# A two-layer graph network on one NeuronCore: the edge phase in four steps per group, written as functions, with the phases that follow it reordered

## The reference, cut to what matters

```python
def L0(V, E, edge_index):            # 8 heads of 16
    Q, K, Vv = V[src] @ Wq + bq, V[dst] @ Wk + bk, V[dst] @ Wv + bv
    scores = einsum(Q, K) / 4 + (E @ Wb + bb)
    alpha = exp(scores - segment_max(scores, dst)[dst]) / segment_sum(...)[dst]
    return segment_sum(alpha * Vv, dst) @ Wo + bo
def L1(x, W, a, edge_index):
    h = x @ W
    e = leaky_relu((h @ a1)[src] + (h @ a2)[dst], 0.2)
    return segment_sum(softmax(e)[:, None] * h[src], dst)   # one softmax over all edges
x = layernorm(x + L0(x, edge_attr, edge_index))
x = layernorm(x + L1(x, W, a, edge_index))
```

## Time and profile before

| | |
|---|---|
| median of 3 executions | 1305.71 us (1303.69 to 1308.90) |
| profiled execution | 1310.51 us, its span 1308.8 us |
| granted clock of PE | 0.737 |
| busy: PE, DVE, ACT, POOL | 733.0, 776.4, 703.8, 787.1 us |
| moved by DMA | 196.96 MB, 150 GB/s on the mean |
| edge phase, second phase, third phase | to 675, to 981, to 1309 us |

### The profile page before, as it was taken

The page is one execution under the profiler, slowest core; times in us unless marked ns, Lnnn a source line. Parts: engine busy times, 40 slices in busy tenths (PEclk is TensorE's granted clock), DMA queues, the critical chain, the costliest instruction groups (busy, mean ns, idle before and its releaser), DMA issues.

```text
span 1308.8 us, 16204 instructions
## 1 busy us (share of the span) xinstructions
PE 733.0 (56%) x3263; PEld 501.9 (38%) x3263; DVE 776.4 (59%) x4008; ACT 703.8 (54%) x2047; POOL 787.1 (60%) x803
## 2 busy tenths in 40 slices
PE   2167767766766676677524555455456453453540
PEld 1045555545544454555524445455452111111110
DVE  2367667776766776678734555555527565464651
ACT  0257767767777687688512333333355454354542
POOL 7677666666766676660036665566643666556665
PEclk9577787778778877877756776777767666666775
DMA  5246556565465655656143767767643222222210
GB/s 138 67 124 209 179 182 198 168 226 176 155 215 181 195 172 179 206 164 234 65 147 119 215 214 213 213 210 221 209 138 121 63 79 71 69 66 71 76 47 26
DMA packets 81840, 196.96 MB, mean 150 GB/s; under 512 B 19746, under 2 KB 21815, under 8 KB 81732
## 3 DMA queue, kind: packets, MB, share of 16 engines
q1 hardware_dynamic: 56558, 148.29, 35.2%
q0 software_dynamic: 25184, 47.65, 12.4%
HBM read 122.71 MB, written 77.22 MB: 153 GB/s over the span
## 4 chain that ended last, share of the span: by engine, by line
ACT 36%; another core or an unknown queue 28%; issue 17%; DVE 12%; PE 6%; POOL 1%; ACTq 0%; POOLq 0%; DVEq 0%
ACT h_res L642 9%; ACT node_out L642 8%; ACT yb L642 7%; DVE node_out L1152 3%; PE psum L599 3%; DVE part L1158 2%; DVE nst L1164 2%; ACT h_res L693 2%; ACT xsT L764 2%; ACT h_res L664 2%; ACT h_res L745 1%; PE psum L606 1%; ACT h_res L651 1%; ACT xsT L740 1%
## 5 line engine op out<-in xcount | busy, mean ns | idle before, releaser
L442 POOL DMA_INDIRECT out_dram<-yb,at_last x196 | 195.0, 995 | 134.6 <-ACT yb L642 75.3
L438 POOL DMA_INDIRECT xs<-in_x,src_tab x196 | 187.1, 955 | 126.1 <-remote 76.0
L438 POOL DMA_INDIRECT xs<-x_all,row_tab x196 | 187.4, 956 | 111.4 <-remote 56.4
L438 POOL DMA_INDIRECT h_res<-in_x,dst_tab x196 | 212.4, 1084 | 59.7 <-issue 59.7
L532 PE MATMUL psum<-xsT,h_res 128*128 128x512 f32 x98 | 93.2, 1051 | 155.0 <-ACT h_res L693 155.0
L627 PE MATMUL psum<-node_out,ident_inv 128*128 128x512 f32 x98 | 80.8, 919 | 149.1 <-DVE node_out L1152 105.3
L642 ACT ACTIVATE h_res<-node_in,shift,rstd 128x128 f32<-128x128 f32 (+1 forms) x392 | 155.8, 486 | 6.3 <-DVE shift L907 3.6
L599 PE MATMUL psum<-w,xsT 128*128 128x129 f32 x392 | 85.5, 386 | 110.3 <-ACT xsT L740 109.7
L740 ACT ACTIVATE xsT<-psum 128x512 f32<-128x512 f32 x49 | 29.3, 597 | 206.6 <-remote 125.5
L599 PEld LDWEIGHTS psum<-w,xsT 128*128 128x128 f32 x392 | 75.8, 287 | 118.5 <-ACT xsT L740 116.7
L642 ACT ACTIVATE yb<-psum,shift,rstd 128x128 f32<-128x128 f32 x196 | 73.8, 457 | 67.4 <-remote 33.5
(11 more groups left out here) (253 smaller groups left out, 1988.5 us busy)
## 6 DMA issues: line engine op xcount, KB each, us to landing
x1d_in<-x_all SPq DMA_DIRECT2D x98, 256.0 KB
node_in<-in_x SPq DMA_DIRECT2D x48, 512.0 KB
x_all<-h_res SPq DMA_DIRECT2D x48, 512.0 KB
out_dram<-node_out SPq DMA_DIRECT2D x48, 512.0 KB
x_all<-yb SPq DMA_DIRECT2D x49, 256.0 KB
src_b<-src_t SPq DMA_DIRECT2D x49, 256.0 KB
node_in<-x_all SPq DMA_DIRECT2D x24, 512.0 KB
h_res<-in_edge_attr SPq DMA_DIRECT2D x7, 784.0 KB
```

The lines of the kernel that those rows point to most:

```text
L438: return pool.indirect_dma_start(out=to, out_offset=None, in_=table, in_offset=bass.IndirectOffsetOnAxis(ap=idx, axis=0))
L442: return pool.indirect_dma_start(out=table, out_offset=bass.IndirectOffsetOnAxis(ap=idx, axis=0), in_=rows, in_offset=None, bounds_check=l ...
```

## The change

The loop over steps with its offsets is taken apart into functions, one for each piece of work, and every engine's order is written anew. A group takes four steps: in step s its transposes, q, k, queries, products, values and scores; in s+1 maxima, exponentials, sums, shares and weighted transposes; in s+2 outputs, addition and bn_stats; in s+3 bn_aggr, logarithm, shift and scaling. The number of bn_aggr stays: 4 rows and 8 of a node chunk, twelve in a step. Node chunks run 3 steps ahead of the groups (`FIRST` = -3), the bias for them lies in PSUM, chunk 0 is moved by two transfers (96 and 10 partitions). The transposes signal `xs_T` and `xd_T` apart, and POOL waits for `xs_T`. Scaling into `node_out` is cut into halves of 4, over two steps, in the first and the second phase. The fix chain is written out between the last groups' operations. LEAD becomes 3. In the second phase PE makes a group's row counts ahead of its transposes. In the third a group's kept sums move into its own step, the moments of s-1 stand in one block, and ACT weighs two groups ahead.

```diff
-    LEAD = 6
-    DRAIN = 7
-    XS, XD, XDT, YB, NI, NX, NO, SB, XI = 4, 8, 4, 4, 3, 3, 2, 7, 4
+    LEAD = 3
+    AHEAD = 5
+    FIRST = 2 - AHEAD
+    XS, XD, XDT, YB, NI, NX, NO, SB, XI = 4, 8, 2, 4, 3, 3, 2, 7, 4
...
-        return k % 2 == 1
+        return k > 0 and k % 2 == 0
...
+        bo_all = bank[4][:, 384:384 + D]
...
@@ POOL @@
-                wait(pool, xT_done, g - XS + 1)
+                wait(pool, xs_T, g - XS + 1)
...
@@ PE, the edge phase @@
+            for s in range(GROUPS):
+                turn_dst(s)
+                if edge(s - 2):
+                    outputs(s - 2)
+                turn_src(s)
+                keys_and_queries(s)
+                values(s)
...
+                if edge(s - 1):
+                    turn_weighted(s - 1)
+                scores(s)
...
+            for r in range(LEAD):
+                rows_of(r)
             for s in range(GROUPS + 1):
...
                     last.then_inc(h_mm, 1)
+                if s + LEAD < GROUPS:
+                    rows_of(s + LEAD)
                 if edge(s):
...
                     last.then_inc(x1_T, 1)
-                if s + LEAD < GROUPS:
-                    rows_of(s + LEAD)
...
@@ ACT, the edge phase @@
+            for s in range(FIRST, GROUPS):
...
+                if edge(s):
+                    copy_dst(s)
+                if edge(s - 1):
+                    weights(s - 1)
+                if s - 3 >= -AHEAD:
+                    deviations(s - 3)
+                if edge(s):
+                    copy_src(s)
+                out_half(s - 4 + AHEAD - 1, 1)
+                out_half(s - 4 + AHEAD, 0)
+                if edge(s):
+                    queries(s)
+                if edge(s - 3):
+                    apply_rows(s - 3)
...
+                if edge(s - 1):
+                    copy_weighted(s - 1)
+                if edge(s - 3 + AHEAD):
+                    apply_nodes(s - 3 + AHEAD)
...
@@ ACT, the second phase @@
-                j = s // 2 - 1
-                if s % 2 == 0 and 0 <= j < len(LATE):
+                j = s // 2
+                if j < len(LATE):
...
-                    scale_rows(node_out[:, j % NO, :], node_in[:, j % NI, :], P, ROWS, ratio[:, LATE[j], :], None)\
+                    scale_rows(node_out[:, j % NO, :], node_in[:, j % NI, :], P, HALVES[s % 2], ratio[:, LATE[j], :], None)\
...
@@ ACT, the third phase @@
+            weigh(0)
+            weigh(1)
+            for s in range(GROUPS):
+                act.wait_ge(e_var, s + 1)
...
+                if edge(s + 2):
+                    weigh(s + 2)
+                act.wait_ge(e_shift, s + 1)
...
@@ DVE, the edge phase @@
+            for s in range(FIRST, GROUPS):
+                if edge(s):
+                    attr_products(s)
+                if edge(s - 1):
+                    score_rows(s - 1)
+                if edge(s):
+                    attr_sums(s)
+                if edge(s - 1):
+                    maxima(s - 1)
+                    exp_args(s - 1)
+                if s - 3 >= -AHEAD:
+                    variances(s - 3, (lambda: carry_max(s)) if s > 0 else None)
+                if edge(s - 2):
+                    add_rows(s - 2)
+                if edge(s - 1):
+                    sums(s - 1)
+                    carry_sum(s)
+                    shares(s - 1)
+                if s - 3 >= -AHEAD:
+                    shifts(s - 3)
+                if edge(s - 2):
+                    row_moments(s - 2)
+                if edge(s - 2 + AHEAD):
+                    bias_nodes(s - 2 + AHEAD)
+                if edge(s):
+                    products(s)
+                if edge(s - 2 + AHEAD):
+                    node_moments(s - 2 + AHEAD)
...
+            def bias_nodes(k):
...
+                v.tensor_tensor(rows, rows, bo_all[0:n, :].unsqueeze(1).to_broadcast([n, ROWS, D]), ALU.add)\
+                    .then_inc(node_biased, 1)
+            def variances(b, between=None):
...
+                if edge(b):
+                    dve.wait_ge(y_stats, b + 1)
                     for t in range(G):
+                        last = v.bn_aggr(nmv[:, t, :], nst[:, t, :])
+                if edge(b + AHEAD):
...
+                    for r in range(G, NR):
+                        last = v.bn_aggr(nmv[0:n, r, :], nst[0:n, r, :])
+                last.then_inc(var_done, 1)
...
@@ DVE, the second phase @@
             for s in range(GROUPS):
-                if s + LEAD + 1 < GROUPS:
-                    reach_of(s + LEAD + 1)
-                dots_of(s)
                 if s + LEAD < GROUPS:
                     rows_at(s + LEAD)
-
+                if s + LEAD + 2 < GROUPS:
+                    reach_of(s + LEAD + 2)
+                dots_of(s)
...
@@ DVE, the softmax: all columns but the last group's ahead of the last h_kept @@
+            lead = slice(0, (GROUPS - 1) * G)
...
@@ DVE, the third phase @@
-            for s in range(GROUPS + 3):
-                a, b, i = s - 1, s - 2, s - 3
+            for s in range(GROUPS + 2):
+                if edge(s):
...
+                    running(s, 0)
+                i = s - 2
...
+                if edge(s):
+                    running(s, 1)
...
+                    running(s, 2)
+                    running(s, 3)
...
+                b = s - 1
                 if edge(b):
...
+                if edge(s):
+                    kept(s, 0)
                 if edge(b):
...
+                    for t in range(G):
+                        last = v.bn_aggr(emv[:, b % 2, t, :], nst[:, t, :])
+                    last.then_inc(e_var, 1)
+                if edge(s):
+                    for t in range(1, G):
+                        kept(s, t)
```

More of the change, by code:

```diff
@@ L495, in rows_of, with outputs @@
+            def outputs(g):
+                pe.wait_ge(hv_turned, g + 1)
+                wait(pe, y_done, g)
+                if g == 0:
+                    pe.wait_ge(prep_act, 3)
+                add_bias(bank[6], 1)
+                for t in range(G):
+                    last = mm(tile(bank[6], t), tile(hT[:, g % 2, :], t), wo[:, :], start=False, stop=t == G - 1)
+                last.then_inc(o_mm, 1)
             def rows_of(r):
@@ new lines, in out_half, with queries @@
+            def out_half(k, half):
+                if not edge(k) or late(k):
+                    return
+                n, o = parts(k), out_no(k)
+                act.wait_ge(x1_applied, k + 1)
+                if o >= NO:
+                    act.wait_ge(out_stored[o % NO], out_count(o - NO))
+                scale_rows(node_out[0:n, o % NO, :], node_x1[0:n, k % NX, :], n, HALVES[half], ratio[:, k, :], None)\
+                    .then_inc(out_applied, 1)
+            def queries(g):
+                act.wait_ge(q_mm, g + 1)
+                wait(act, prod_done, g)
+                fn(qT[:, 0, :], bank[2], ACT.Identity, bias=bcol[:, 0:1]).then_inc(q_done, 1)
@@ new lines, in _ @@
+            apply_rows(GROUPS - 1)
+            act.wait_ge(fix_dve, 6)
+            fn(flog[:, :], fmv[:, 1:2], ACT.Ln, bias=eps_cols[:, 0:1]).then_inc(fix_log, 1)
+            act.wait_ge(fix_log, 1)
+            fn(frs[:, 0:1], flog[:, :], ACT.Exp, scale=-0.5).then_inc(fix_act, 1)
+            act.wait_ge(fix_dve, 7)
+            fn(x1f[:, :], yf[:, :], ACT.Identity, bias=frs[:, 1:2], scale=frs[:, 0:1]).then_inc(fix_act, 1)
+            for u in range(NO):
+                act.wait_ge(out_stored[u], out_landed(u))
@@ L737, in _ @@
+            for s in range(GROUPS + 1):
+                g = s - 1
                 if edge(s):
@@ L1103, in dots_of @@
+            dve.wait_ge(fix_act, 6)
+            v.scalar_tensor_tensor(frs[:, 1:2], fmv[:, 0:1], -1.0, frs[:, 0:1], ALU.mult, ALU.mult).then_inc(fix_dve, 1)
+            for r in range(LEAD):
+                rows_at(r)
+                reach_of(r + 2)
             def dots_of(g):
```

1032 lines of the change are left out of this document (504 added, 528 removed).

## The result

The changed kernel took 1357.41 us (median of 4 executions, 1352.73 to 1364.0) against 1305.01 for the kernel before: a ratio of 1.040, 95% interval 1.035 to 1.045. It is slower by 4%, where I forecast 2% faster (1279). The time lies between rival 1's 1335 and 1391. The profiled execution took 1364.0 us, its span 1362.3.

The account below looks back on a forecast made before the run. No engine was taken as full; a closed loop of POOL's burst, late release of PE's results and next burst sets the pace. Terms -27 - 3 - 30 + 40 - 3 - 4 = -27 gave 1279 us, range 1215 to 1365.

Parts of the forecast that it names:

- rival 1: Edge phase: chain inside a step meets the held release, 2.5 us per period; 1391, or 1335 in every second; chance 0.28.
- the gather beside the bias addition: Edge phase: bias operand from PSUM shortens one gather per group by 0.6 us over 45 periods, 27 us less.
- the end of the edge phase: Last edge gather to second phase: one group remains instead of six more steps, 30 us less, bounds 21 and 40.
- the start: Before the steady edge phase: loads only reordered, four groups fit before POOL needs a transpose; -3, bounds +10 and -11.
- the softmax: Between second and third phase: most logits taken early, reciprocals moved later; -3 us, bounds 0 and -4.
- (a): Edge phase: a step's chain from transposes to scores costs nothing, covered by node scaling and bn_stats; otherwise rival 1.
- (b): Edge phase: release follows POOL's burst, so a shorter gather shortens the period to 11.4 us; 27 us less.
- rival 2: Second phase: rows don't gate, 1239 to 1229; with the edge phase at POOL's pace too, 1160; chance 0.16.
- (c): Second phase: with LEAD 3 row tables gate POOL, 7.2 us per group against 6.25; +40, bounds -10 and +100.
- The third phase: Third phase: loop drops one step at its end, scatters stay the floor; -4 us, bounds -40 and +15.
- parts 1 and 4: Steady edge phase, 27 us less, and second phase, 40 more; both rest on a release that follows POOL's bursts.
- unseen PE work: Edge phase: the 4 us after PE's estimated end could be PE working; then the 27 us term would be zero.

Follow-up runs that it names:

- the second chip: Changed kernel repeated unaltered against the kernel before on a chip with late results: 1392.8 against 1318.5 us, ratio 1.059.
- src_first_c: Changed kernel with PE's source transposes ahead of the outputs of two groups back, slower chip: 1315.5 us, ratio 1.010 to the kernel before.
- psum_bias: Kernel before with only the bias addition's second operand read from PSUM, prompt chip: 1099.0 us against 1132.0.
- all3_b: Changed kernel with source transposes ahead of outputs, weighted transposes ahead of values, LEAD = 5, slower chip: 1295.5 us, ratio 0.996 to the kernel before.
- before_c: Kernel before, unchanged, run for its trace on a prompt chip: span 1122.7 us.
- after_d: Changed kernel, unaltered, as control on a prompt chip: 1067.3 us, span 1064.4.

## Why the prediction was wrong, and where it was right

On prompt chips several terms came out as priced: the gather beside the bias addition -27 (measured -25 in the edge phase from group 10, and -29 to -33 as an edit by itself), the end of the edge phase -30 (-26.3), the start -3 (-4.1), the softmax -3 (-3.2). For the first of these that is luck: I had argued it by the loop with the late release, and there it holds because POOL never pauses. On the chip of the result the end of the edge phase (-23.5) and the softmax (-2.1) came near, and the sum failed by three steps.

**(a) "Unheld I cost this at nothing."** In the sum I costed the chain inside a step at nothing and put its price into rival 1, at 0.28. The trace of before showed results held in every period. So the work was not unheld, and the rival was the case to expect. Measured were 13.09 us per period here and 13.68 on the second chip, +1.10 and +1.66 against the kernel before. Rival 1 stood on top of the forecast's 11.4: 12.65 with its 2.5 us in every second period, 13.9 in every one, so the measured lie between. The mechanism is the one named, and a change of one place in PE's order removed it; but a hit cost some 3.5 us, as the alternation of 12.0 and 15.5 shows, and not 2.5.

**(b) "POOL is in the loop."** I took the release to follow the end of POOL's burst, and so counted the shorter gather as shorter period. The first half holds. The traces also record when a semaphore is updated, which I call the report of a result. I took the 34 periods from group 10 to 44 of the six traces on slower chips. In the kernel before, held results of PE (those reported over 0.3 us after their recorded end) are reported 1.2 to 1.5 us after the end of POOL's last gather in all 68 periods, in the changed kernel and its variants 1.5 to 1.8 us after it in 134 of 136. In 24 of these 136 another held result comes sooner, within 0.5 us of that gather's end, as L570 does in the period shown above. The second half doesn't: the time from the end of a burst to the next burst isn't fixed. In the kernel before (medians) a burst takes 10.27 us, the report comes 1.33 later and POOL starts 0.38 after it, 12.0 in all. In src_first_c they are 9.68, 1.72 and 0.56, again 12.0: the 0.6 us off the burst were lost behind it. Part of that is PE's order, as L536 ends only after the release (recorded at 465.78, ACT's copy at 465.52), while L561 is among what was held. Why the release itself comes 0.4 later I can't say, and whether the gather alone would have brought the 27 us there was not isolated, since psum_bias never met such a chip. For a chip without late results I had only the tail of rival 2, 1160.

**(c) The second phase.** +40, measured +15.4 (+26 on the second chip) and 0 on the prompt kind. The gate was the row table, as forecast, and LEAD = 5 removes it. But only part of the chain of 5 us stands in POOL's way: in the period shown PE's row products had been passed on earlier, DVE's lookup (L994) began at 755.10, 1.4 us before ACT's copy, and POOL started 0.9 us after that copy began. The term was mis-sized: 0.3 us per group (0.5 on the second chip), not 0.8.

The start was a smaller miss: -3, bounds -11 and +10, measured +13.7 (+12.1 on the second chip). I had said that four groups fit before POOL needs a transpose, which is so (group 4 began at 46.0 us against 46.5), but put nothing on the wait behind it, 15.3 us for L536. src_first_c and all3_b brought back part of it; what else delays the first steps is open.

The third phase's +11.2 (I had -4) I can't explain. On the second chip it was 305.3 us against 301.2, +4.1, on prompt chips -0.2, and in src_first_c and all3_b 307.1 and 308.5 us. POOL's waits for ACT's scaling grew by as much, from 75.3 to 86.0 us, but no experiment changed the order of this phase.

I also said that a release which doesn't follow POOL's bursts would take the ground from parts 1 and 4. Where there is a late release in the edge phase, it does follow them. On four chips there was none: part 4 then cost nothing, and part 1 came in full.

The Trainium skill's page "Perfetto Trace Analysis", section on the Tensor Engine instruction, says that PE's end is an estimate, and I asked whether the 4 us could be unseen PE work. The runs speak against it: the same instruction list, at a granted clock of 0.737 and 0.760, has the gap on the one kind of chip and not on the other, and DVE is held with PE (last section). psum_bias gained 29 to 33 us by moving one operand to PSUM; the Trainium skill's page "SBUF — State Buffer", section on the two separate sides, by which two SBUF inputs of DVE exclude a GpSimd operation that reads SBUF, agrees.

## What to carry to other kernels

If a trace shows a wait whose releaser had long ended, don't take the delay as a constant: ask which results would be late if they were delayed in the new order, and keep what the bounding engine waits for first in its producer's list, ahead of anything that needs a second hand-over. Putting an operation that only feeds the far end of the pipeline ahead of the one that refills it cost nothing here where hand-overs are prompt. Where they are not it cost some 3 to 5%, an estimate from the ratios 1.040 and 1.059 of the changed kernel against 1.010 of src_first_c on another chip. Measure on more than one chip before a change of order is judged.

## What the runs showed of the hardware

The experiments name six chips; that of the result is not named and may be a seventh. On four (the prompt kind) the kernel before took 1123 to 1132 us, on the others (the slower kind) 1296 to 1320. Durations of instructions are nearly the same on both (a gather 0.94 us, ACT's copies 0.58 to 0.60); what differs is when results are passed on.

On the slower kind PE's results come late from the second half of a burst of gathers on. In the earlier trace rows L561 is recorded as ended at 309.84 and ACT copies at 313.94, 4.1 us later. The reports show the same in all 34 periods of that trace: the outputs (L551) are reported 4.2 us after their recorded end (median, at most 5.1), the transposes L561 3.5, the scores L525 2.5. On prompt chips, in the edge phase of before_c and after_d, every report of PE, DVE and ACT comes within 0.04 us of the recorded end. There POOL waited for PE for 3.0 us in the whole run of before_c, and in after_d for 0.9.

It is not PE alone. DVE's last bn_aggr of a step, in the kernel before, is reported late too, and in 31 periods within 0.05 us of a held result of PE (at 313.79 both, in the earlier trace rows). DVE also stops between bn_aggr for which it waits for nothing. Their group in the kernel before on the slower chip of the earlier trace rows, then in before_c:

```profile
L1028 DVE BATCH_NORM_AGGREGATE nmv<-nst 128x2 f32<-128x6 f32 (+1 forms) x392 | 38.4, 155 | 42.2 <-issue 34.3 <-remote 7.2 <-DVE nst L1016 0.2
```

```profile
L1028 DVE BATCH_NORM_AGGREGATE nmv<-nst 128x2 f32<-128x6 f32 (+1 forms) x392 | 29.8, 146 | 0.5
```

The idle time ahead of them is 42.2 us on the one and 0.5 on the other. ACT's reports in the edge phase come at once in both.

Whether this is the chip or what ran beside it, and what in it holds the results, stays open. That most come through 1.2 to 1.8 us behind POOL's last gather is a pattern in time and not a cause. The test of it, a pause in the burst, met a prompt chip in all three of its runs.
